# Two on-chip moves handed to transfers: the lower value blocks and the token shift of a half tile

## What is computed

```python
def shift_token(t):
    t1, t2 = jnp.split(t, 2, axis=-1)
    t2 = jnp.pad(t2, ((0, 0), (1, 0), (0, 0)))[:, :-1]
    return jnp.concatenate([t1, t2], axis=-1)
...
bk, bv = (look_around(bk), look_around(bv))   # each window of 64 sees itself and the window before
...
x = x + o @ wo
h = shift_token(x)
mu = h.mean(-1, keepdims=True)
var = h.var(-1, keepdims=True)
h = (h - mu) / jnp.sqrt(var + 1e-05) * lg + lb
```

## Time and profile before

| | us |
|---|---|
| median of 3 runs | 2481.74 (2478.46 to 2484.01) |
| the profiled execution | 2479.8 |
| its span | 2478.0 |
| mean granted TensorE clock | 0.979 of full |

### The profile page before, as it was taken

The page is one execution under the profiler, slowest core; times in us unless marked ns, Lnnn a source line. Parts: engine busy times, 40 slices in busy tenths (PEclk is TensorE's granted clock), DMA queues, the critical chain, the costliest instruction groups (busy, mean ns, idle before and its releaser), DMA issues.

```text
span 2478.0 us, 59154 instructions
## 1 busy us (share of the span) xinstructions
PE 2243.9 (91%) x22208; PEld 1567.1 (63%) x22208; DVE 1675.2 (68%) x3612; ACT 1702.9 (69%) x2766; POOL 1771.1 (71%) x1615
## 2 busy tenths in 40 slices
PE   4888999999999999999999999999999999988887
PEld 1454666676666666666676666666666666665665
DVE  3666766777676776777667676677667766556653
ACT  1455677677777777767777776776777777776663
POOL 2117777786877868777777867777777877788883
PEclk9899999999999999999999999999999999999998
DMA  4221001110110110111011001011111100000000
GB/s 136 62 66 53 29 26 29 44 34 20 42 32 27 36 38 27 26 47 33 22 34 42 27 29 38 22 41 36 33 27 31 45 23 19 8 12 12 2 3 12
DMA packets 74966, 81.99 MB, mean 33 GB/s; under 512 B 7545, under 2 KB 64294, under 8 KB 74674
## 3 DMA queue, kind: packets, MB, share of 16 engines
q1 hardware_dynamic: 74674, 78.04, 11.0%
HBM read 56.26 MB, written 20.97 MB: 31 GB/s over the span
## 4 chain that ended last, share of the span: by engine, by line
PE 50%; ACT 18%; DVE 12%; issue 10%; POOL 8%; DMA 1%; SPq 0%; DVEq 0%; ACTq 0%; POOLq 0%
PE ps L540 8%; PE ps L633 6%; PE ps L825 4%; PE ps L588 4%; PE ps L573 3%; PE ps L700 3%; ACT PT L1188 3%; PE ps L739 3%; PE ps L553 3%; PE ps L722 2%; PE ps L816 2%; DVE ss L1027 2%; DVE nmax L976 2%; POOL inv L1407 2%; PE ps L687 2%
## 5 line engine op out<-in xcount | busy, mean ns | idle before, releaser
L976 DVE TENSOR_REDUCE nmax<-ps 128x1 f32<-128x512 f32 (+3 forms) x1024 | 471.6, 485 | 383.2 <-PE ps L575 380.4
L1188 ACT ACTIVATE PT<-ps 128x512 f32<-128x512 f32 (+1 forms) x768 | 407.0, 533 | 327.7 <-PE ps L590 323.3
L1407 POOL TENSOR_TENSOR inv<-ss,nhalf 128x16 f32<-128x16 f32 x128 | 378.7, 2959 | 322.3 <-DVE QN L1010 322.3
L573 PE MATMUL ps<-KA,QA 72*128 72x512 bf16 (+3 forms) x1024 | 290.2, 310 | 38.4 <-DVE nmax L976 33.1
L1396 POOL TENSOR_TENSOR RS<-RAW,rot 128x512 f32<-128x512 f32 x256 | 324.9, 1290 | 0.0
L1402 POOL TENSOR_TENSOR RC<-RC,RS 128x1024 f32<-128x1024 f32 x128 | 304.0, 2375 | 18.9 <-POOL RS L1396 1.3
L1385 POOL TENSOR_TENSOR RC<-RAW,rot 128x1024 f32<-128x1024 f32 x128 | 307.9, 2405 | 0.0
L588 PE MATMUL ps<-QA,KA 75*128 75x512 bf16 (+3 forms) x1024 | 285.6, 305 | 19.5 <-ACT PT L1188 15.4
L687 PE MATMUL ps<-wqkv,ZT 128*128 128x512 f32 x512 | 242.8, 597 | 0.0
L1246 ACT COPY V_odd<-ps 128x512 f32<-128x512 f32 x128 | 74.9, 585 | 217.1 <-PE ps L700 216.5
L1017 DVE TENSOR_REDUCE nm<-ps 128x8 f32<-128x1024 f32 x128 | 156.2, 1220 | 96.1 <-PE ps L722 95.1
(11 more groups left out here) (130 smaller groups left out, 5674.6 us busy)
## 6 DMA issues: line engine op xcount, KB each, us to landing
QA<-parts SPq DMA_DIRECT2D x192, 96.0 KB
KA<-parts SPq DMA_DIRECT2D x192, 96.0 KB
parts<-qkp SPq DMA_DIRECT2D x32, 384.0 KB, 5.5
X_next<-in_x SPq DMA_DIRECT2D x17, 256.0 KB, 2.9
X<-in_x SPq DMA_DIRECT2D x16, 256.0 KB, 3.0
x_kept<-X SPq DMA_DIRECT2D x16, 256.0 KB, 3.0
XR<-x_kept SPq DMA_DIRECT2D x32, 128.0 KB, 3.7
out<-XR SPq DMA_DIRECT2D x32, 128.0 KB, 1.9
```

What stands on the lines that cost most here:

```text
L573: pe.matmul(dst[:, c0:c0 + w], QA[e][0:QK_ROWS, h % UNIT, qt * P:(qt + 1) * P], KA[e][0:QK_ROWS, h % UNIT, 0:w], start=True, stop=False)
L976: ins = v.tensor_reduce(nmax[:, NT - 1 - r, h % H1:h % H1 + 1], for_max(i, x)[:, c0:c0 + w], AX.X, ALU.max, negate=True)
L1188: a.activation(PT1[:, h % UNIT, c0:c0 + w], for_exp(i, x)[:, 0:w], ACT.Exp, scale=SCALE1).then_inc(exped.sem, 1)
L1407: g.tensor_tensor(inv[:, :], ss[:, :], nhalf[:, :], ALU.pow).then_inc(inv_ready.sem, 1)
```

## The change

SP gets two new tasks in every slot. `move_values(s + 1)` waits for ACT's one copy to V_odd and copies rows 0 to 63 and rows 64 to 127 of it into the two V_even buffers; `attend` waits for that. `shift_tokens(s - 1)` waits for z_acc and copies the upper 64 columns of Z, rows 0 to 126, into rows 1 to 127 of XN, and one row from the tile before (or from a row of the identity, whose upper half is zero) into row 0; DVE's new `shifted_tokens` waits for that. PE's two matmuls, DVE's copy and ACT's two half copies go. On DVE, `norms` stands ahead of the wait for the shift and the moments come after `gate_up` and `heads_over_sum`. On POOL, `tile_root` moves behind `rotate_by_sin`.

```diff
+        v_moved = Landed(nc, ctx, "v_moved", 2 * ITEMS)
-        sh_mm = count("sh_mm", ITEMS)
-        sh_ready = count("sh_ready", ITEMS)
+        shifted = Landed(nc, ctx, "shifted", 2 * ITEMS)
...
-                (shift[:, :], t["shift"]), (corner[:, :], t["corner"]),
...
+                def move_values(m):
+
+                    sp.wait_ge(*past(v_ready.sem, v_ready.at(i, m + 1)))
+                    for n, rows in enumerate((slice(0, WIN), slice(WIN, P))):
+                        sp.dma_start(V_even[(m + n) % 2][rows, :, :], V_odd[rows, :, :]).then_inc(v_moved.sem, 16)
+
+                def shift_tokens(m):
+
+                    l, z, tt = place(m)
+                    dst = XN[m // HT % 2][:, m % HT, D // 2:D]
+                    sp.wait_ge(*past(z_acc.sem, z_acc.at(i, m + 1)))
+                    sp.dma_start(dst[1:P, :], Z[z][0:P - 1, tt, D // 2:D]).then_inc(shifted.sem, 16)
+                    first = Z[z][P - 1:P, tt - 1, D // 2:D] if tt else ident[0:1, D // 2:D]
+                    sp.dma_start(dst[0:1, :], first).then_inc(shifted.sem, 16)
...
+                    if tile_in(i, s - 1):
+                        shift_tokens(s - 1)
                     if s % 2 == 0:
                         u = s // 2 + 10
                         if unit_in(i, u):
                             lay_maxima(u)
                         if unit_in(i, u + 2):
                             lay_out(u + 2)
+                    if tile_in(i, s + 1):
+                        move_values(s + 1)
...
                 def attend(m):
                     pe.wait_ge(*past(pt_ready.sem, pt_ready.at(i, m + 1)))
-                    pe.wait_ge(*past(v_ready.sem, v_ready.at(i, m + 1)))
+                    pe.wait_ge(*past(v_moved.sem, v_moved.at(i, 2 * (m + 1))))
...
                     if tile_in(i, s - 1):
-                        pe.wait_ge(*past(sh_ready.sem, sh_ready.at(i, s)))
+                        pe.wait_ge(*past(z_acc.sem, z_acc.at(i, s)))
...
                     pe.wait_ge(*past(on_ready.sem, on_ready.at(i, m + 1)))
-                    pe.wait_ge(*past(sh_ready.sem, sh_ready.at(i, m)))
+                    pe.wait_ge(*past(z_acc.sem, z_acc.at(i, m)))
...
-                def shift_tokens(m):
-                    l, z, tt = place(m)
-                    pe.wait_ge(*past(z_acc.sem, z_acc.at(i, m + 1)))
-                    dst = m_ps[:, D:D + D // 2]
-                    mm = pe.matmul(dst, shift[:, :], Z[z][:, tt, D // 2:D], start=True, stop=(tt == 0))
-                    if tt:
-                        mm = pe.matmul(dst, corner[:, :], Z[z][:, tt - 1, D // 2:D], start=False, stop=True)
-                    mm.then_inc(sh_mm.sem, 1)
...
+                    v.wait_ge(*past(x_tr.sem, x_tr.at(i, m // HT - 1)))
                     v.wait_ge(*past(wo_mm.sem, wo_mm.at(i, m + 1)))
...
                 def tokens(m):
                     l, z, tt = place(m)
-                    xn = XN[m // HT % 2][:, m % HT, half:D]
-                    v.wait_ge(*past(x_tr.sem, x_tr.at(i, m // HT - 1)))
-                    v.wait_ge(*past(sh_mm.sem, sh_mm.at(i, m + 1)))
-                    v.tensor_copy(xn, m_ps[:, D:D + half]).then_inc(sh_ready.sem, 1)
+                    v.wait_ge(*past(z_acc.sem, z_acc.at(i, m + 1)))
                     v.bn_stats(stats[z][:, tt, 0:6], Z[z][:, tt, 0:half])
-                    v.wait_ge(*past(sh_ready.sem, sh_ready.at(i, m + 1)))
-                    v.bn_stats(stats[z][:, tt, 6:12], xn).then_inc(tile_stats.sem, 1)
+
+                def shifted_tokens(m):
+                    l, z, tt = place(m)
+                    v.wait_ge(*past(shifted.sem, shifted.at(i, 2 * (m + 1))))
+                    v.bn_stats(stats[z][:, tt, 6:12], XN[m // HT % 2][:, m % HT, half:D]).then_inc(tile_stats.sem, 1)
 
                 def tile_moments(m):
                     l, z, tt = place(m)
                     v.wait_ge(*past(tile_stats.sem, tile_stats.at(i, m + 1)))
-                    if tile_in(i, m + 4):
-                        norms(m + 4)
-                    else:
-                        v.tensor_copy(spare[:, 0:1], nhalf[:, 0:1])
+                    v.tensor_copy(spare[:, 0:1], nhalf[:, 0:1])
...
                     attention_step(s, 3)
+                    if tile_in(i, s + 3):
+                        norms(s + 3)
                     if tile_in(i, s - 1):
-                        tile_moments(s - 1)
-                    elif tile_in(i, s + 3):
-                        norms(s + 3)
+                        shifted_tokens(s - 1)
                     if b:
                         gate_up(p, 0)
                         gate_up(p, 1)
                     if s % 2 and unit_in(i, (s + 17) // 2):
                         heads_over_sum((s + 17) // 2)
+                    if tile_in(i, s - 1):
+                        tile_moments(s - 1)
...
                     a.wait_ge(*past(v_mm.sem, v_mm.at(i, m + 1)))
-                    a.copy(V_odd[:, :, 0:E2], heads)
-                    a.copy(V_even[m % 2][0:WIN, :, 0:E2], heads[0:WIN, :, :])
-                    a.copy(V_even[(m + 1) % 2][WIN:P, :, 0:E2], heads[WIN:P, :, :]).then_inc(v_ready.sem, 1)
+                    a.wait_ge(*past(v_moved.sem, v_moved.at(i, 2 * m)))
+                    a.copy(V_odd[:, :, 0:E2], heads).then_inc(v_ready.sem, 1)
...
                         rotate_by_cos(s + 2)
+                    if tile_in(i, s + 2):
+                        rotate_by_sin(s + 2)
                     if tile_in(i, s - 1):
                         tile_root(s - 1)
-                    if tile_in(i, s + 2):
-                        rotate_by_sin(s + 2)
                     if tile_in(i, s - 1):
                         tile_normalise(s - 1)
```

More of the change, by code:

```diff
@@ L192, in build @@
         band = sb("band", [P, 2, P], BF16)
-        shift = sb("shift", [P, P])
-        corner = sb("corner", [P, P])
         cos1 = sb("cos1", [P, S])
@@ L391, in build @@
         y_out = landed("y_out", LANES)
-        N_FIRST, N_CONST = 4, 12 + L * 7
+        N_FIRST, N_CONST = 4, 10 + L * 7
         N_MADE = LANES + 9
@@ L853, in body @@
                     attention_step(s, 2)
-                    if tile_in(i, s - 1):
-                        shift_tokens(s - 1)
                     if tile_in(i, s):
@@ L1457, in constants @@
         "one_row": np.ones((1, HS), f),
-        "shift": np.eye(P, k=1, dtype=f), "corner": ((q == P - 1) & (k == 0)).astype(f),
         "ones": np.ones((SPLIT, UNIT * S), bf),
```

## The result

The changed kernel takes 2463.21 us, median of 6 runs (2456.93 to 2467.24). The kernel before took 2483.28 us beside it (6 runs), ratio 0.9925, 95% interval [0.9903, 0.9948]. So it is faster, by 0.75%, which is clear of the noise: about 19 us where 69 were forecast, and its time lies a microsecond above the range. The interval of a gain is 4 to 7 us wide to either side, and a difference of two gains is good to some 7 to 9 us.

What follows compares the result with a forecast made beforehand. PE's queue was taken to bound the interior, the POOL-DVE ring the tail. 41 + 25 + 5 + 8 = 79, less 10, gave 69: 2413 us. Forecast range 2375 to 2445 (0.62); with A, 2375 to 2462.

Steps and rivals of the forecast that it cites:

- PE's 41 us: Shift's matmuls leaving PE: 0.385 us a slot, all on PE's path in 108 interior slots, nothing in the tail.
- rival D: Whole kernel: no change, as other waits take up PE's freed time at once; chance 0.04.
- the 90 that were named as a sign of being right: PE over the whole run: busy time down by some 90 us if the forecast was right.
- The root behind the rotation, 5 + 8 us: POOL no longer idles for the variance: 5 us at one place between slots 7 and 8, 8 us in the tail.
- The values, 25 us: Two of three value copies leave ACT, shortening PE's wait ahead of L633 in odd slots: 25 us, bounds 16.3 to 74.
- The transfers, nothing: Values' moves land in some 3.5 us, the shift 3.9 us after z_acc; both cost nothing.
- the lower of the bounds: Shift's rows in single file: 14 to 29 ns a packet, so 1.8 to 3.7 us; 20 ns, 2.5 us taken.
- A: Rival: half the gain, shift's packets at 29 ns land late for `gate_up`; gain 34, time 2448; chance 0.20.
- B: Rival: slower, shift's packets at 45 ns land 7.0 us after z_acc; time 2688; chance 0.09.
- the three signs named for a wrong forecast: DVE's shift wait over 1 us a slot; PE waiting for V_even's transfer; PE's row-maxima waits up by over 20 us.
- The giving back, 10 us: An eighth of the 79 us sum given back, as other relays end later than PE in a few slots.
- the relays next in line: Row maxima that PE waits for and ACT's step 0 exponential after `values`, ending later than PE in a few slots.

Runs made afterwards that it cites:

- run 1116: Not a follow-up run: the longest duration, 1116 ns, of DVE's clamp instruction in the kernel before, where its median was 175 ns.

## Why the prediction was wrong

**PE's 41 us** (`all of it on PE's path`). This step failed on this kernel: put back, the same matmuls cost 14 us. They cost 33 once DVE's clamp is out of the way, and 40 to 50 without the edge's stall. The evidence given against rival D, matmuls in flight in 95% of the interior, did not carry: the interior was at 94% after as well (813.60 of 870). PE's busy time as a whole fell by 38 us (2243.9 to 2205.7), not by the 90 that were named as a sign of being right: the 90 are durations of instructions that overlap others on PE.

**The root behind the rotation, 5 + 8 us.** In the interior the gain is there and larger. Slot 8, from tile 7's addition to tile 8's, is 2.6 us shorter in the mean over the second to the seventh body, 16 us, and with the root back in its old place it is as long as before. In the tail it isn't: from tile 107's addition to the last it is 278.6 us before and 276.1 after, and with the clamp on POOL 272.4 and 273.1. What failed most is that the step priced only what waits for the root. The root fills POOL's gap, and it was in this gap that DVE's clamp ran in 0.17 us. The rows for it were at hand: the clamp's median before was 175 ns, its longest run 1116. Price: the change is worth 45 us with the clamp on POOL and 19 with it on DVE, so 26. This is the same loss as that of PE's step, seen from the other side, and not one more.

**The values, 25 us.** Mechanism right (the wait ahead of `values` went from 16.3 to 2.7), size off: 15 us with the clamp on POOL, good to some 9, near the lower bound; 10 with the clamp in the way.

**The transfers, nothing.** Right on this kernel, in part by luck. Each of the two moves of V_even landed 2.6 us after its issue, so both in some 3.2 us (forecast: about 3.5), and PE never waited for them. The shift's packets came at 14 ns in one file, the lower of the bounds (20 was taken): the first 1.3 us after the issue, the last 3.1. In the last tiles DVE goes on 3.9 us after z_acc's end, just as forecast, but because two errors cancel: the rows took 1.8 us and not 2.5, and the 0.8 us from the last row to DVE's start was in no term. DVE waited 15.5 us in all, and 0.9 ahead of the last four tiles, where A and B needed 0.5 us and more in each slot. But with the clamp out of the way it waits in most even slots, 0.5 to 0.6 us without the clamp and about 0.3 with the clamp on POOL: those for which the forecast saw 0.5 us to spare. Of the three signs named for a wrong forecast none came: PE's waits for row maxima grew by 10 us, not 20. The sign that came had not been named: `gate_up` late for PE with no late transfer ahead of it.

**The giving back, 10 us.** It was to come from the relays next in line; it came from there in part. Not foreseen was the place of PE's instructions: 13 us on the changed kernel, where the kernel before had 6 to give as well.

Added up: 69 forecast, less 26 for the clamp, 10 for the values, 7 to 13 for the edges, leaves 20 to 26; measured 19. What is left is within the intervals, but the parts were measured on different kernels and depend on each other, so the sum is an estimate. With the clamp on POOL and the instructions moved, the changed kernel is at 2403.19 us, 62 us under the kernel before with the clamp on POOL. That 62 is near the 69 forecast is in part a coincidence: the values were 10 short, and the partner ran without the waits, which no term had and which bring 6 on the kernel before. That version leaves out no part of the computation and beats both kernels, the changed one by 59 us by the gains.

## What to carry to other kernels

An idle stretch on one engine may be where another engine's instruction gets through: before you fill a gap on POOL, look what DVE runs beside it, and in which form. A small group whose longest instruction is many times its usual one (1116 and 175 ns here) may be held by something: look whether its long runs end with an instruction of another engine, as they did here, before that engine gets busier. If a change in a long unrolled loop gains less than it should, compare the slots at the loop's jump; a run with some satisfied waits ahead of the loop can tell whether the place of the instructions has a part in it. Run it on the kernel before too.

## What was not expected of the hardware

- A 16-column tensor_scalar on DVE lasted 174 to 3437 ns in one kernel, each long one ending within 0.04 us of a POOL instruction; as a tensor_reduce over twice the data it lasted 185 to 188.
- It goes both ways: where DVE's two-input addition started 0.05 us ahead of POOL's, it kept its 0.69 us and POOL's took 2.85 us instead of about 2.35.
- PE stopped for 1.85 to 2.02 us early in a row of 32 matmuls, with no wait in the records, at four loop jumps, each time beside a 16 KB block of a queue of kind "instruction". With 64 or 128 satisfied waits ahead of its loop this stall was gone, and 13 to 17 us in all.
- 127 rows of 256 B went in one file at 14 ns each, 1.8 us; 112 rows were through in about 0.25 us.
